# Decoder kernel, convolution stage: half of the gather transfers begun on ScalarE's queue instead of SyncE's

## The reference

```python
shift_k = irfft(rfft(k_kernel) * rfft(k))[..., :L]
k = shift_k + k_D * k
kv = k * v
y = irfft(rfft(kv) * rfft(ssm_kernel))[..., :L]
y = y + kv * D
return (y * q) @ Wo.T + bo
```

## Time and profile before

| | |
|---|---|
| runs before | 5124.71 us median of 3 (5123.08 to 5126.34) |
| profiled execution | 5094.72 us, span 5092.6 us |
| TensorE busy | 4820.7 us (95%), mean granted clock 0.978 |
| VectorE busy | 2856.6 us (56%) |
| ScalarE busy | 1659.0 us (33%) |
| convolution stage | from about 2165 us to about 2650 us of the span |

### The profile page before, as it was taken

How to read it: one execution, slowest core, us unless ns; L and a number is a source line. 1 busy time by engine, 2 the same in 40 slices (tenths; PEclk the granted TensorE clock), 3 DMA queues, 4 the chain that set the end, 5 groups by cost and what they waited for, 6 DMA issues and landing times. The chain is left out here.

```text
span 5092.6 us, 124764 instructions
## 1 busy us (share of the span) xinstructions
PE 4820.7 (95%) x49200; PEld 2866.0 (56%) x49200; DVE 2856.6 (56%) x4880; ACT 1659.0 (33%) x2033; POOL 1701.6 (33%) x1428
## 2 busy tenths in 40 slices
PE   9999989989999989989979899879999999999998
PEld 4444445658887756533334566545566565555555
DVE  4244236766554345465652567656666666666665
ACT  1001005544323210045431344234434334333333
POOL 1001004645554411100002234435545454454543
PEclk9999999989999999999989999989999999999999
DMA  1000011141111233397866211136667667899996
GB/s 61 9 33 25 9 60 50 64 117 43 41 34 33 75 111 100 122 245 200 223 198 255 76 59 43 53 119 223 223 201 241 227 229 262 307 316 327 314 321 198
DMA packets 446626, 743.99 MB, mean 146 GB/s; under 512 B 119905, under 2 KB 236390, under 8 KB 439860
## 3 DMA queue, kind: packets, MB, share of 16 engines
q1 hardware_dynamic: 330240, 695.01, 39.8%
q0 software_dynamic: 36160, 43.09, 4.2%
q10 hardware_dynamic: 79988, 2.67, 1.0%
HBM read 559.39 MB, written 107.88 MB: 131 GB/s over the span
## 5 line engine op out<-in xcount | busy, mean ns | idle before, releaser
L3557 PE MATMUL ex_ps<-ex_w,ex_xT 128*32 128x256 f32 x20992 | 1169.1, 380 | 36.7 <-DVE ex_w L3458 33.0
L3557 PEld LDWEIGHTS ex_ps<-ex_w,ex_xT 128*32 128x32 f32 x20992 | 681.9, 110 | 496.3 <-DVE ex_w L3458 52.0
L3458 DVE COPY ex_w<-ex_shelf 128x4096 f32 x328 | 750.7, 2289 | 290.5 <-PE ex_ps L3557 109.1
L3515 ACT ACTIVATE ex_w<-ex_shelf 128x4096 f32 x164 | 594.0, 3622 | 688.8 <-PE ex_ps L3569 606.8
L3569 PE MATMUL ex_ps<-ex_w,ex_hT 128*32 128x256 f32 x10496 | 599.4, 380 | 5.8 <-ACT ex_w L3515 5.8
L3421 POOL DMA_INDIRECT out<-ex_y,ex_ix_out x164 | 326.3, 1990 | 778.1 <-DVE ex_xT L3445 300.1
L3404 POOL DMA_INDIRECT ex_x<-moe_xn,ex_ix x328 | 533.9, 1628 | 137.7 <-issue 99.1
L3569 PEld LDWEIGHTS ex_ps<-ex_w,ex_hT 128*32 128x32 f32 x10496 | 343.8, 110 | 231.9 <-ACT ex_w L3515 6.2
L2888 POOL TENSOR_TENSOR go_xb<-go_xr,go_bias 128x2048 f32<-128x2048 f32 x8 | 38.2, 4778 | 626.4 <-DMA go_xr<-x 560.1
L634 PE MATMUL at_ps<-at_xT,at_kT 128*128 128x512 f32 (+3 forms) x640 | 239.3, 529 | 1.6 <-ACT at_kT L528 1.6
L3520 ACT ACTIVATE ex_g<-ex_ps 128x512 f32<-128x512 f32 x164 | 98.1, 598 | 400.0 <-issue 400.0
(11 more groups left out here) (366 smaller groups left out, 8013.4 us busy)
## 6 DMA issues: line engine op xcount, KB each, us to landing
ex_shelf<-L_ffn_w SPq DMA_DIRECT2D x128, 2048.0 KB
ex_shelf<-L_ffn_wo SPq DMA_DIRECT2D x64, 2048.0 KB
cv_gt<-cv_g SPq DMA_DIRECT2D x320, 128.0 KB, 2.6
cv_vt<-cv_v SPq DMA_DIRECT2D x256, 128.0 KB, 3.3
ff_x<-x SPq DMA_DIRECT2D x16, 1024.0 KB
ex_raw_x<-slot_token ACTq DMA_DIRECT2D x656, 0.5 KB
at_low<-x SPq DMA_DIRECT2D x8, 1024.0 KB, 8.3
x<-at_acc SPq DMA_DIRECT2D x8, 1024.0 KB, 4.2
```

The source lines that it names most:

```text
L3458: dve.tensor_copy(w_s[n][:, :], pick(shelf[n], buf)).then_inc(w_set[n].sem, 1)
L3515: act.activation(w_s[2][:, :], pick(shelf[2], buf), ACT.Copy).then_inc(w_set[2].sem, 1)
L3557: mm = pe.matmul(ps[r * LANES:(r + 1) * LANES, which, hh * FL:(hh + 1) * FL], xT[:, p % 2, k, hh * LANES:(hh + 1) * LANES], wu[which][:, k ...
```

## The change

Gathers of odd q (1 and 3) are begun by ScalarE right behind its own v copy; those of even q (0 and 2) stay with SyncE, at the place they had. Bytes, buffers and semaphores are the same.

```diff
+        def gather(eng, n, q):
+            e = seg_of[n]
+            if e >= 2:
+                eng.wait_ge(aux_mm, unit_at["join", step_of[e - 2], 3] + 1)
+                st.plain(eng)
+            eng.wait_ge(v_set, seg_group(n, q))
+            st.plain(eng)
+            for a in range(4):
+                r = 4 * (q % 2) + a
+                eng.dma_start(vt[PLACE[r]:P:UN, e % 2, q // 2], v1[:, q % 2, a, :]).then_inc(vt_in[e % 2][q], 16)
...
-            def gather(n, q):
...
                 for q in range(4):
-                    if slot_back(n, q):
-                        gather(*slot_back(n, q))
+                    if slot_back(n, q) and slot_back(n, q)[1] % 2 == 0:
+                        gather(sp, *slot_back(n, q))
...
                         act.activation(v1[:, bq % 2], ps[:, VB:VB + 4, 0:CW], ACT.Copy).then_inc(v_set, 1)
+                        if bq % 2:
+                            gather(act, bn, bq)
                     for a in slot_units[n, q]:
                         take(a)
```

## The result

The changed kernel takes 5159.2 us, the median of 4 runs (5155.5 to 5165.2), against 5125.0 for the kernel before: a ratio of 1.0070, 95% interval 1.0055 to 1.0085, that is 28 to 44 us slower. Its profiled execution took 5162.5, with a span of 5160.5.

The account below looks back on a forecast made before the run. It took the convolution stage as bound by two close clocks, TensorE with ScalarE (23.0 us a step) and SyncE's issues (about 24.5). Relief -24, ScalarE stall +37.8 and slow clock +9 gave +22.8 us, 5147.5; range 5120 to 5176.

Parts of the forecast that it names:

- the likeliest case: The forecast itself, whole kernel: +22.8 us, 5147.5; chance 0.55, from about 5125 to 5170 by itself.
- Relief of SyncE, -24: Convolution stage: eight of 32 small transfers a step leave SyncE's full queue, late gathers vanish, 24 us won (lower bound 12).
- Stall of ScalarE's issue, 14 x D: Slot 0, q = 3: issuing delays the split copies and TensorE 14 times; 37.8 us lost, 28 to 60 by the bounds.
- D: Time ScalarE needs to issue one gather's four transfers, with restart: 2.7 us, bounds 2.0 to 4.3.
- q = 1 hidden: Slot 2: ScalarE's 16 issues of q = 1 gathers fit before its next needed copy; cost 0.
- The clock, 9: TensorE behind its new stalls: slow clock after every second one, 7 x 1.3 = 9 us; ends 0 and 38.
- The sum: Whole kernel: -24 + 37.8 + 9 = +22.8 us.
- 30 us between profile and runs: Whole kernel before: profiled execution 5094.7 against median 5124.7; the difference was put on the median, giving 5147.5.
- ScalarE's issues hold nothing up: Rival, slot 0: issues run beside the split copies, 24 us won and 0 to 10 paid, 5101 to 5111; chance 0.10.
- Break-even: Rival: a gather's issue on ScalarE takes about 2.0 us and the clock stays up, +4, 5129; chance 0.15.
- DMA engines limit convolution 0: Rival, convolution 0: DMA engines are the limit, only 12 us recovered, +35, 5160; chance 0.12.
- Taking turns at the generator: Rival: SyncE's and ScalarE's queues alternate, ScalarE's four issues stretch towards 4.9 us, 22 us more, +45, 5170; chance 0.08.

Follow-up runs that it names:

- e1: Changed kernel with only the q = 1 gathers begun by ScalarE, those of q = 3 back on SyncE; 0.9971 of the kernel before.
- e3: Changed kernel with the odd-q gathers begun by GpSimd instead of ScalarE; 0.9968 of the kernel before.
- e2: Changed kernel with only the q = 3 gathers begun by ScalarE, those of q = 1 back on SyncE; 1.0134 of the kernel before.
- e6: Changed kernel, but ScalarE begins two of the four transfers of each q = 3 gather and SyncE the other two; 1.0011 of the kernel before.
- e8: Changed kernel with SyncE's 1 MB store of convolution 1 moved from slot 3 to slot 1 of the next step; 1.0083 of the kernel before, one run.
- e7: Changed kernel with four unused matmuls added behind the second split in each of the 14 stall slots; 1.0054 of the kernel before.
- e5: The kernel before, profiled a second time with no edit; 5098 us on that chip, stretch from first to last v copy 441.0 us.
- e10: Changed kernel with the gathers of q = 1 and 2 begun by ScalarE, those of q = 0 and 3 by SyncE; 0.9973 of the kernel before.
- e9: Changed kernel, but ScalarE begins the odd gathers behind the slot's unit copies instead of in front of them; 1.0018 of the kernel before.

## Why the prediction was right

The forecast was 5147 us, +22.8; measured were +34 (28 to 44), inside the range, in the likeliest case and with its sign. The mechanism was right; the size owes something to a wide range, for all three terms of the sum erred to the same side, and the stretch grew by 41.9. By its steps:

- *Relief of SyncE, -24.* The regular gaps returned to 253 us as counted: the 33 gaps of q = 1 to 3 in the eleven later segments sum to 189.3, 33 x 5.74. Short were the gaps behind hat steps (67.8 against 71.2, so 3.4 won for 5.1; the gaps in front of their q = 2 copies are 2.8 longer) and the end (1.2 lost for 1.3 won). Altogether about 20.4. e1 and e3 show the relief by itself: 16 to 21 us of stretch.
- *Stall of ScalarE's issue, 14 x D.* The place, the count of 14 and the mechanism were right: e1, e2 and e6 move the loss with the slot and with the length. D was put at 2.7. The undisturbed one is 2.51 and 0.1 on either side, 2.8 by the gap, and five of the 14 are longer (3.25 to 4.43), three of them beside the store (e8). Sum 40.7 + 14 x 0.32 = 45.2 us instead of 37.8. This term was short by 7.
- *q = 1 hidden.* Right in eleven of the 16 slots of the changed kernel, which stay at 5.70. Behind the four hat steps the cover did not hold: the z0 copy waits 2.8 to 3.4 us for the issue, and the gaps are 0.3 to 0.9 longer than before. Twice TensorE's spectrum waits 0.6 us for it; the other two are longer because the back runs at half clock there (2.01 us for 1.12). So the issue costs 1 to 2 us where 0 was taken. The last gap (6.32) is shorter than it was (7.04).
- *The clock, 9.* It cost 17.0 (e7). I had taken every second stall, seven, at 1.3 us. Nine of the 14 were followed by slow work: six of the eleven inside the runs of segments, and all three over a hat step. Each cost 1.4 to 2.7 us (10.18 - 8.55, and 12.34 less a regular slot and its issue), 1.9 in the mean. So both the count and the price were low. I had also taken all stalls as 2.5 us long; four were 0.8 to 1.7, and of the ten others nine were slow.
- *The sum*: -20.4 + 45.2 + 17 = +41.8, for a stretch that grew by 41.9. The terms close it, within the 3 us by which two executions differ.
- *30 us between profile and runs.* I laid it on the median. The changed kernel doesn't have it: its profiled execution is 3 us above its median, and profile against profile the difference is 68 us, of which 27 lie behind the last v copy. By e5 (profiled execution 5096.6, runs of the kernel before on that chip 5098.2) it is no effect of profiling; that it is one of the chip fits the three groups above, but the chips of the first profile and of the first runs were not compared.

The rivals: that ScalarE's issues hold nothing up is out (2.71 us of idle put down to issue). Break-even would have needed D = 1.5 with the clock up; e6, at 1.75, is close to it and reads 1.0011. That DMA engines limit convolution 0 is out: e1 and e3 recover the time there. Taking turns at the generator is mostly out. In the changed kernel four issues of ScalarE beside a spread took 2.5 to 3.2 us instead of 2.5, and a spread of eight beside them 5.7 to 6.9, where the others took 5.1 to 6.2. Each is stretched by a third at most, not by two. The Trainium skill (Perfetto Trace Analysis, DMA Instruction - HWDGE) says that the descriptor generator is locked for exclusive use; if a whole issue were under that lock, two queues' issues would double where they overlap, and this trace does not show that. The other rule of the Trainium skill's same page (DMA Optimizations), that spreading DMAs over issuing engines may help where descriptor generation is the bottleneck, holds for q = 1 (e1) and for GpSimd (e3), and fails for the kernel as changed, since the engine that was given the work had none of it to spare in slot 0.

## What to carry to other kernels

A transfer is begun in the order of its engine's program, at about 0.6 us each here, and whatever stands behind it waits that long: before moving transfers to a compute engine, look which of its instructions feed TensorE within that time, and put the issues only into slots where it idles (here slot 2 of ScalarE, which e10's slot 3 did not improve on, or an engine with nothing to do). Full queue and full engine are different bounds; the relief was real (16 to 21 us), and the bill of 62 us was paid elsewhere. And a stall of 2.6 us has a second price behind it, in the clock, which was here 17 us: nine of the ten stalls of 2.58 us or more had slow work behind them, and none of the four shorter ones.

## What the runs showed of the hardware

- Behind stalls of TensorE the granted clock fell to the 1.2 GHz level by their length, in the same program: in the changed kernel behind nine of ten of 2.58 to 4.5 us and none of four of 0.8 to 1.7; in e2 behind all 14 of 2.6 to 6.0; in e6 behind those of 2.57 and 2.27 and none of 1.8 or less; in e7, where matmuls that nobody reads fill part of the stall, behind none (2.07 at most left idle). It is no sharp line: e8 has one of 2.78 with full clock behind it, and e9 one of 1.93 with slow splits.
- A 1 MB store begun 0.9 to 1.8 us earlier on SyncE's queue lengthens two or three of ScalarE's next four issues, by 0.6 to 2.0 us together, though it is on the other queue (4.43 against 2.97 without it, 3.46 against 2.50); begun 2.6 us earlier it did little or nothing (2.50 twice, 2.76 once).
- GpSimd begins a 128 KB transfer between SBUF partitions in 0.53 us, less than SyncE's 0.60 and ScalarE's 0.63 (medians). The slowest landing was 10.9 us there (e3), and from 5.4 (e1) to 12.2 us (e8) where only the other two begin them.
